# The pass between two graph layers worked off tile by tile inside the first layer

## The reference, cut to what matters

```python
xn = layernorm(x)                                  # 6250 nodes x 256
g  = gat_conv(xn, W1, al1, ar1, src, dst)          # 8 heads x 64: out = sum(alpha * feat[src])
g  = elu(g)
g  = gat_conv(g, W2, al2, ar2, src, dst)           # 1 head x 256
x  = x + g + linear_attention(xn)                  # 8 heads x 32, Wq, Wkv, Wproj
x  = x + experts(layernorm(x))                     # 8 experts, gated, each 256-256-256-256
```

## Time and profile before

| | us |
|---|---|
| runs | 3202.43, 3200.71, 3200.45 |
| median | 3200.71 |
| the profiled execution | 3202.88 |
| its span | 3200.66 |
| layer one, first to last ring block | 342 to 1619 |
| last ring row's end to layer two's first instruction | 1618.97 to 1810.69 |
| layer two and experts | 1811 to 3200.7 |

### The profile page before, as it was taken

One profiled execution on the slowest core, in us unless ns is written; L12 is line 12 of the kernel. 1 busy time (PEld: TensorE's weight loads), 2 busy tenths in 40 slices (PEclk: granted clock), 3 DMA queues, 4 the chain that ended last, 5 costly groups with the idle time before them and its releaser, 6 DMA issues. The chain is left out here.

```text
span 3200.7 us, 33647 instructions
## 1 busy us (share of the span) xinstructions
PE 2077.2 (65%) x7292; PEld 1320.4 (41%) x7292; DVE 2254.6 (70%) x5492; ACT 1905.1 (60%) x6229; POOL 2091.5 (65%) x1989
## 2 busy tenths in 40 slices
PE   6900355565554455544448400889999999999999
PEld 4700233333333333333336300455555556555665
DVE  6883699999998888888866443666666666666622
ACT  2400688888886766777747332656666566666632
POOL 2417777777777777777437677777777777777200
PEclk9955666676765555555569755899999999999999
DMA  7510899999999999999855466666666666666400
GB/s 228 158 23 12 309 370 378 376 376 376 372 361 374 371 356 361 359 376 360 335 159 133 108 224 203 219 204 211 201 207 209 209 203 218 205 212 200 145 21 13
DMA packets 242083, 779.02 MB, mean 243 GB/s; under 512 B 69020, under 2 KB 116977, under 8 KB 215225
## 3 DMA queue, kind: packets, MB, share of 16 engines
q0 software_dynamic: 124960, 364.74, 35.7%
q1 hardware_dynamic: 86843, 391.15, 32.0%
q10 hardware_dynamic: 30078, 20.99, 2.6%
HBM read 399.48 MB, written 378.12 MB: 243 GB/s over the span
## 5 line engine op out<-in xcount | busy, mean ns | idle before, releaser
L1468 POOL DMA_INDIRECT e_rows<-scratch_table,k_src x1664 | 1740.9, 1046 | 553.8 <-issue 342.0
L1601 ACT ACTIVATE e_rows<-e_rows 128x64 f32<-128x64 f32 (+1 forms) x4160 | 1190.3, 371 | 3.4
L1578 DVE SCALAR_TENSOR_TENSOR e_ring<-e_ring,k_same,e_rows 128x520 f32<-128x520 f32 (+1 forms) x1560 | 967.3, 620 | 258.0 <-ACT e_rows L1601 174.2
L2175 PE MATMUL e_p_y<-e_wfo,e_h 128*121 128x256 f32 x1664 | 391.9, 390 | 44.0 <-DVE e_y L1961 44.0
L2175 PEld LDWEIGHTS e_p_y<-e_wfo,e_h 128*121 128x121 f32 x1664 | 313.9, 190 | 139.0 <-issue 78.1
L2149 PE MATMUL e_p_a<-e_xt,e_wf 128*128 128x484 f32 x832 | 357.6, 573 | 0.7 <-ACT e_xt L2103 0.7
L2161 PE MATMUL e_p_b<-e_h,e_wf 128*128 128x484 f32 x832 | 357.2, 572 | 0.0
L2088 ACT ACTIVATE e_h<-e_p_a,e_shift,e_scale 128x484 f32<-128x484 f32 x208 | 155.3, 752 | 243.3 <-PE e_p_a L2149 243.3
L1004 PE MATMUL e_p_kv<-e_wkv,nd_feat 128*121 128x512 f32 x208 | 183.6, 1034 | 111.3 <-DVE nd_feat L909 110.6
L1961 DVE SCALAR_TENSOR_TENSOR e_y<-e_p_y,e_w,e_y 121x256 f32<-121x256 f32 x416 | 180.8, 476 | 101.2 <-PE e_p_y L2175 101.0
L1547 DVE TENSOR_TENSOR e_rows<-e_rows,e_shared 128x4096 f32<-128x4096 f32 x52 | 229.7, 4417 | 18.5 <-ACT e_rows L1594 18.2
(11 more groups left out here) (416 smaller groups left out, 3414.7 us busy)
## 6 DMA issues: line engine op xcount, KB each, us to landing
scratch_rows_a<-e_ring SPq DMA_DIRECT2D x104, 2112.0 KB
scratch_rows_b<-e_ring SPq DMA_DIRECT2D x104, 1032.0 KB, 4.5
e_rows<-scratch_table,k_src POOLq DMA_INDIRECT x1664
scratch_table<-na_frow ACTq DMA_DIRECT2D x52, 245.8 KB
scratch_table<-hi_frow ACTq DMA_DIRECT2D x52, 124.8 KB
na_x<-in_x SPq DMA_DIRECT2D x13, 484.0 KB
e_wkv<-in_x SPq DMA_DIRECT2D x52, 121.0 KB
scratch_res<-e_wkv SPq DMA_DIRECT2D x52, 121.0 KB
```

The lines of the kernel that those rows point to most:

```text
L1468: nc.gpsimd.indirect_dma_start(out=rows[:, n % B, g, :], out_offset=None, in_=table, in_offset=bass.IndirectOffsetOnAxis(ap=k.src[:, n * G ...
L1578: nc.vector.scalar_tensor_tensor(ring[:, i, j - c0, 0:W + H], prev, k.same[:, n * G + j:n * G + j + 1], rows[:, rb, j, 0:W + H], ALU.mult, ...
L1601: last = nc.scalar.activation(rows[:, rb, j, at], rows[:, rb, j, at], ACT.Copy, scale=rows[:, rb, j, W + h:W + h + 1])
L2175: last = nc.tensor.matmul(self.p_y[bank][0:BK, i * D:(i + 1) * D], self.h2[:, e % 2, kt, v:v + BK], self.wfo[:, e, kt, :], start=kt == 0, ...
```

## The change

`hidden_pass` is gone. A new class `Hidden`, held by `Mixing`, does the same work for each tile, in the order of the periods (a tile may start once its period's sums are stored), in three parts:

- 36 tiles inside blocks 33 to 51: one tile a block in 33 to 38, 40 and 41, three a block in 42 to 50 (slots 0, 1, 2), one in 51. With `AT` = 2, 7, 12 for the slots, DVE takes the share (reciprocal) at j = AT, the mean one row later, the negative part two, the elu six rows later; ACT the exponent and relu at AT + 4, the turned tile at AT + 9, the two copies out at AT + 12; where that passes 16 it falls into the next block. POOL issues gathers at j = 3, 8, 13 and the scatters of three blocks ago at j = 5, 10, 15. On PE the transposes and products stand between the attention's steps, as the diff shows. SP stores a tile's rows in the next block, ahead of the ring's first half.
- 12 tiles (`LATE`) after the last ring row, among the steps of the last period's tail.
- 4 tiles (`LAST`) after that tail's store has landed.

The reciprocal is of one tile's eight numbers, and mean and flag are one instruction, in place, in a ring of eight row buffers. These, the weights W2 and the rows to store lie where node features lay that the attention has already weighed. One pair of buffers (`ex`) holds first the exponents of a tile, then its transposes; `negative(i)` waits until tile i-2 is multiplied. `shared` has one PSUM bank for two. W2 and its vectors are loaded by SP in block 30, its extra columns made by DVE in block 31. `er2` is written by periods. The 26 copies of the order move from layer two's start to the end of `index_pass`'s DVE work.

The diff, cut to its core:

```diff
+            for q in range(Q):
+                first = dve.value_load(k.block[0:1, 0, q:q + 1], min_val=0, max_val=NB - KB)
+                c(V.tensor_copy(k.order[:, :, q * KB:(q + 1) * KB], k.index[:, :, bass.ds(first, KB)]))
+                c(V.tensor_copy(k.with_edges[:, q * KB:(q + 1) * KB], k.has[:, bass.ds(first, KB)]))
...
                 self.weigh(pe, t0)
+                hidden.product(pe, n - 1, 1)
                 if q is not None:
                     tails.tensor_turn(pe, q)
+                hidden.transposes(pe, n - 1, 2)
                 self.turn_back(pe, t0)
                 if q1 is not None:
                     tails.tensor_spread(pe, q1)
                 if q is not None:
                     tails.tensor_back(pe, q)
                 self.output(pe, t0)
+                hidden.product(pe, n - 1, 2)
                 self.weigh(pe, t1)
+                hidden.transposes(pe, n, 0)
                 if q is not None:
                     tails.tensor_sum(pe, q)
                 self.turn_back(pe, t1)
                 self.output(pe, t1)
+                hidden.product(pe, n, 0)
+                hidden.transposes(pe, n, 1)
         tails.tensor_turn(pe, Q - 1)
         tails.tensor_back(pe, Q - 1)
-        tails.tensor_sum(pe, Q - 1)
+        for i in hidden.LATE + hidden.DRAIN:
+            if i == hidden.LATE[2]:
+                tails.tensor_sum(pe, Q - 1)
+            hidden.tensor_stage(pe, i, hidden.LATE)
+        for i in hidden.LAST + hidden.END:
+            hidden.tensor_stage(pe, i, hidden.LAST)
...
+        hidden, tails = self.hidden, self.tails
+        tails.vector_scan(dve, Q - 1)
+        for i in hidden.LATE + hidden.DRAIN:
+            if i == hidden.LATE[1]:
+                tails.vector_shift(dve, Q - 1)
+            if i == hidden.LATE[2]:
+                tails.vector_scale(dve, Q - 1)
+            if i == hidden.LATE[3]:
+                tails.vector_join(dve, Q - 1)
+            hidden.vector_stage(dve, i, hidden.LATE)
+        tails.vector_top(dve, Q - 1)
         for part in range(3):
-            self.tails.vector_merge(dve, Q - 1, part)
+            tails.vector_merge(dve, Q - 1, part)
+        for i in hidden.LAST + hidden.END:
+            hidden.vector_stage(dve, i, hidden.LAST)
...
+class Hidden:
+    BATCH = [33, 34, 35, 36, 37, 38, 40, 41] + [n for n in range(42, 51) for i in range(3)] + [51]
+    SLOT = [0] * 8 + [i for n in range(42, 51) for i in range(3)] + [0]
+    AT = (2, 7, 12)
+    LOOP = len(BATCH)
+    DONE = NB - KB
+    LATE = list(range(LOOP, DONE))
+    DRAIN = [DONE, DONE + 1]
+    LAST = list(range(DONE, NB))
+    END = [NB, NB + 1]
+    RING = 8
...
+        self.rows = flat[0:BK, self.base:self.base + self.RING * L1.row].rearrange("p (i n) -> p i n", i=self.RING)
+        self.prod = mixing.early[:, 0:4 * D].rearrange("p (k n) -> p k n", k=4)
+        self.ex = mixing.early[:, 0:4 * D].rearrange("p (i n) -> p i n", i=2)
...
+    def share(self, dve, i):
+        b = i % self.RING
+        dve.wait_ge(self.rows_in[b], 16 * (i // self.RING + 1))
+        wait(dve, self.agg_ready, i - 1)
+        self.nc.vector.reciprocal(self.rec[:, i % 2, :], self.rows[:, b, L1.den:L1.max]).then_inc(self.rec_ready, 1)
+
+    def mean(self, dve, i):
+        b = i % self.RING
+        by_head = "p (h e) -> p h e"
+        row = self.rows[:, b, 0:512].rearrange(by_head, h=8)
+        dve.wait_ge(self.rec_ready, i + 1)
+        self.nc.vector.scalar_tensor_tensor(row, row, self.k.with_edges[:, i:i + 1], broad(self.rec[:, i % 2, :], L1.dim),
+                                            ALU.mult, ALU.mult).then_inc(self.agg_ready, 1)
+
+    def negative(self, dve, i):
+        if i < 2:
+            dve.wait_ge(self.wlr_ready, 1)
+        else:
+            dve.wait_ge(self.f_ready, i - 1)
+        dve.wait_ge(self.agg_ready, i + 1)
+        self.nc.vector.tensor_scalar(self.ex[0:BK, i % 2, :], self.rows[:, i % self.RING, 0:512], 0.0, None, ALU.min
+                                     ).then_inc(self.neg_ready, 1)
+
+    def elu(self, dve, i):
+        row = self.rows[:, i % self.RING, 0:512]
+        dve.wait_ge(self.ex_ready, i + 1)
+        self.nc.vector.scalar_tensor_tensor(row, self.ex[0:BK, i % 2, :], -1.0, row, ALU.add, ALU.add).then_inc(self.hid_ready, 1)
...
+    def vector_stage(self, dve, i, tiles):
+        if i in tiles:
+            self.share(dve, i)
+            self.mean(dve, i)
+            self.negative(dve, i)
+        if i - 1 in tiles:
+            self.elu(dve, i - 1)
+
+    def scalar_stage(self, act, i, tiles):
+        if i in tiles:
+            self.exponents(act, i)
+        if i - 1 in tiles:
+            self.turned(act, i - 1)
+        if i - 2 in tiles:
+            self.out(act, i - 2)
+
+    def tensor_stage(self, pe, i, tiles):
+        if i - 2 in tiles:
+            self.multiply(pe, i - 2)
+        if i - 1 in tiles:
+            self.turn(pe, i - 1)
...
-        shared = [s.ps(f"shared{i}", [P, 512]) for i in range(2)] if AH < H else None
+        shared = s.ps("shared", [P, 512]) if AH < H else None
...
-def hidden_pass(nc, a, k):
...
-        for q in range(Q):
-            first = dve.value_load(k.block[0:1, 0, q:q + 1], min_val=0, max_val=NB - KB)
-            c(nc.vector.tensor_copy(self.index[:, :, q * KB:(q + 1) * KB], k.index[:, :, bass.ds(first, KB)]))
-            c(nc.vector.tensor_copy(self.has[:, q * KB:(q + 1) * KB], k.has[:, bass.ds(first, KB)]))
...
-            hidden_pass(nc, a, k)
```

More of the change, by code:

```diff
@@ L861, in __init__ @@
         self.res_out = s.sems("res_out")
+        self.hidden = Hidden(nc, a, k, s, self, stored)
     def tiles(self, n):
@@ L881, in sync @@
         t = self.tiles(n)[half]
+        if half == 0:
+            self.hidden.sync(sp, n)
         if n == self.HALF - 1:
@@ L890, in sync_last @@
     def sync_last(self, sp):
+        self.hidden.sync(sp, NB)
         self.tails.sync_fix(sp, Q - 1)
+        for i in self.hidden.LATE:
+            self.hidden.store(sp, i)
         self.tails.sync_out(sp, Q - 1)
+        for i in self.hidden.LAST:
+            self.hidden.store(sp, i)
+        self.hidden.sync_last(sp)
         for i in range(2):
@@ L957, in vector @@
                 self.quotient(dve, t1)
+        self.hidden.vector(dve, n, j)
     def exponents(self, act, t):
@@ L993, in scalar @@
                 self.residual(act, t1)
+        self.hidden.scalar(act, n, j)
     def project(self, pe, t):
@@ L1054, in tensor @@
     def tensor(self, pe):
-        tails = self.tails
+        tails, hidden = self.tails, self.hidden
         for n in range(NB):
@@ L1407, in edge_pass @@
         work = work_of(nc, a, k, s, tails, stored)
-        shared = [s.ps(f"shared{i}", [P, 512]) for i in range(2)] if AH < H else None
+        shared = s.ps("shared", [P, 512]) if AH < H else None
         shared_ready = s.sem("shared_ready")
-        def share(b):
-            return shared[b][:, 0:H * G1].rearrange("p (h j) -> p h j", h=H)
+        share = shared[:, 0:H * G1].rearrange("p (h j) -> p h j", h=H) if AH < H else None
         block = s.block()
@@ L1590, in _ @@
                 if AH < H:
-                    nc.scalar.activation(shared[b][:, 0:H * G1], d[:, :, :].rearrange("p h j -> p (h j)"), ACT.Exp
+                    nc.scalar.activation(shared[:, 0:H * G1], d[:, :, :].rearrange("p h j -> p (h j)"), ACT.Exp
                                          ).then_inc(shared_ready, 1)
@@ L1790, in __init__ @@
         R = L2.row
-        self.index = s.sb("index", [BK, 2, NB], I32)
-        self.has = s.sb("has", [BK, NB])
         self.wf1 = s.sb("wf1", [P, E, 2, D])
@@ L1935, in vector_first @@
         c.done()
-        nc.vector.sem_inc(self.ordered)
         for i in range(2):
@@ L1982, in shares @@
         c.done()
-        c(nc.vector.tensor_tensor(rec[:, :], rec[:, :], self.has[:, g * KB:(g + 1) * KB], ALU.mult))
+        c(nc.vector.tensor_tensor(rec[:, :], rec[:, :], self.k.with_edges[:, g * KB:(g + 1) * KB], ALU.mult))
         c.done()
@@ L2275, in gps_kernel @@
         k.has = k.sb("has", [BK, NB])
+        k.order = k.sb("order", [BK, 2, NB], I32)
+        k.with_edges = k.sb("with_edges", [BK, NB])
         k.block = k.sb("block", [P, 2, Q], I32)
```

361 lines of the change are left out of this document (202 added, 159 removed).

## The result

The changed kernel takes 3223.59 us as the median of six runs (3208.01 to 3225.83), against 3205.64 for the kernel before in its six: a ratio of 1.0045, 95% interval 1.0024 to 1.0067. It is slower by 0.45%, and the interval does not reach down to 1; 3175 us within 3142 to 3216 was forecast. The profiled execution is the shortest of the six, 3208.01 us with a span of 3206.2, so the changed kernel was profiled a second time among the experiments (3219.07 us, span 3217.3; there the median of ten runs was 3217.59 and the ratio 1.0039, 1.0023 to 1.0055).

A forecast was written before the change was run, and what follows sets the result against it. DVE's ring steps were taken to bound layer one's second half, DMA close behind; nothing was full in the hidden stage. 3202.9 - 86.7 (tail gain) + 61 (longer blocks) - 2.2 (profile to median) gave 3175 us, range 3142 to 3216.

The forecast's parts named there:

- what is removed: Old hidden stage between the last ring row and layer two's first instruction: 191.7 us, all on the path.
- the edits at nothing: Moved order copies (some 11 us, hidden by other engines in the index pass), single `shared` bank, shifted gathers and scatters: no cost.
- The new tail: Last ring row to layer two: four-engine chain, 4.55 us a tile, 105 us in all (98 to 140), gain 86.7.
- The blocks: Blocks 42 to 50 get longer by 44.5 us, to 30.2 a block from 25.2, by DVE's work and PE's third product.
- All near, none above: In blocks 42 to 50, POOL (27.9 us a block), DMA (26.8 to 28.7) and ACT (24) stay under 30.2.
- The sum of DVE's prices: Per tile in the blocks, DVE's added operations cost 1.36 us after gaps between ring rows; bounds 1.0 and 2.05.
- The other terms: Eight one-tile blocks 8.8 us longer, block 31 with the weights 4, block 51 4.
- the signs that were to show it wrong: Forecast is wrong if blocks 42 to 50 pass 32 us each or the tail passes 120.
- (a): Rival: PE's clock stays low in blocks 42 to 50 (78 us longer) and tail (up to 140): 3243 us, chance 0.22.
- (b): Rival: gaps between ring rows can't be used, DVE pays 2.05 us a tile: 3200 us, no change, chance 0.13.
- (c): Rival: blocks take only POOL's 27.9 us, DVE's slack swallows the rest: 3154 us, or 3143; chance 0.17.
- The rule on GpSimd's lock: DVE's negatives in a two-port mode would hold POOL 1.4 us more a block, 29.3, still under 30.2.

The follow-up runs named there:

- the run with buffers alone: Changed kernel with two buffers of their own for the tail's turned tiles, order of stages as before: 3181.00 us in one run.

## Why the prediction was wrong

**What bounds, and what is removed.** The 191.7 us were all on the path. The cover named for the edits at nothing held. The copies of the order take 10.8 us at the end of the index pass, DVE's wait there falls from 53.22 to 41.80, and layer one's first ring row comes at 347.05 where it came at 347.51. With no tile in the blocks layer one is within 4 us of the kernel before from block 31 on, block 31's weights (3.8) among them.

**The new tail: the step that failed most.** The chain was named, and its two lengths were right to 0.05 us: 4.55 a tile at the full clock (4.50 measured), 6.8 at half (6.82). What failed is the choice between them: "I add 3 because PE comes into the tail at half clock", 105 us, as if the clock rose by itself after the first tiles. In the second profile's chain PE works 5.05 of 6.82 us and its granted clock is 0.57 over the tail; in the first the two lengths alternate at 0.73: 130.7 and 113.7. The start was right, the fourth negative at E+18.1 to 18.2 for E+17.3; the eight cycles behind it took 53.5 and 42.6 us for 36.4. The hidden stage of before had 0.90, but there two buffers at each step let PE run ahead; the new tail has one pair. The runs show it from both sides: kept busy by empty transposes, PE ran the very same chain at 4.50; with the chain cut it took 2.37 to 3.16 a tile. The gain was 61.0 to 78.0 instead of 86.7. In the second profile that is 25.7 of the 42 us by which the sum was off, in the first 8.7 of 27.5, less than the blocks' 10.5. The Trainium skill, page "TensorE: Matmul & The Clock Gate", section "Loop structure matters more than you think", says that the loop nest decides whether matmuls stay at the high clock. The traces agree in part: 0.57, 0.85 and 0.82 for the second profile's chain, the chain with PE kept busy and the chain cut; but the unchanged chain also ran at either level, 4.50 and 6.82 us a tile.

**The blocks: 55 instead of 44.5.** DVE's busy time grew by 42.7 us, 1.58 a tile where 1.36 was taken (+5.9), and its idle time by 12.3 where 7.8 was taken (+4.5). The place of the wait, weigh(t1) behind the third product, was right: moving the product gave 11 us back. Its size was near, 7.3 more at the quotient for 7.8: the third product took 3.98 us in five of eight blocks and 2.10 in three, 3.3 in the mean where 2.9 was taken. What was put at nothing is DVE's wait for the rows that ACT scales: ACT was priced by its busy time, 24 us a block, "All near, none above", and DVE's wait for it grew from 4.5 to 14.0. What the prediction also did not see is that DVE, PE and POOL end these blocks within a few us of one another. One more operation on DVE costs 0.19 at most instead of 0.41, since waits give way, while 24 more gathers on POOL cost 26 of their 34 us. The sum of DVE's prices was no bound.

**The other terms.** Blocks 31 to 41 took 14.4 to 17.6 for 12.8, block 51 5.2 to 8.3 for 4. The lengthening in all was 77.6 to 80.0 (with the later start of block 31) for 61: within its bounds of 40 and 110, but with the tail it turned the sign. Of the signs that were to show it wrong, the blocks stayed under 32 (31.3 in the mean) and the wait at the quotient under 4 (3.3 at the longest); the tail passed 120 in the second profile.

**The rivals.** (a) was half right: its place in the blocks and its tail at low clock are what the runs show, with the blocks' clock at 0.67, over the 0.6 that it named, and 55 instead of its 78. So 3224 came out, between the forecast and its 3243. (b) falls: an added operation cost less than the price taken. (c) falls as it was worded; POOL needed 30.9 a block and not 27.9. The rule on GpSimd's lock, named beside the sum, shows nowhere here but is not excluded: layer one's gathers took 1120 ns in the mean without negatives beside them and 1087 and 1110 in the two profiles with 27 of them; a run that changes the negatives alone was not made.

## What to carry to other kernels

Before a stage is taken apart, ask what its own rate would be where it goes: here a tile cost 2.04 us inside the blocks and 2.4 to 2.9 in a pipelined tail, so the saving lay between these, and a tail that lost its double buffers threw it away. A chain through four engines must be priced at both levels of PE's clock, here 4.50 and 6.82 us a tile, and not at the clock of the stage it comes from. When a block has three engines within a few per cent of its length, price the added work on each queue by the mean of rows in that company, not by the shortest row.

## What the runs showed that was not expected

The same instructions at the same buffers settle in two lengths, 4.50 and 6.82 us a tile, and both appear in one kernel: the first profile's tail alternates (its negatives 40 to 47 are 5.25 apart in the mean), the second stays at 6.8. PE's busy share is 74% of the time both in the second profile's chain (5.05 of 6.82 us) and with the empty transposes (3.35 of 4.50), so these rows give no rule for it. What decides which length a run of the unchanged kernel gets was not tried. In the blocks it shows as well: block 46 took 28.0 us at a clock of 0.76 in the first profile and 31.3 at 0.67 in the run with buffers alone, with the same code in the blocks. And 96 transposes that nobody reads, in a stretch of 130 us, made it 28 us shorter.
